# Group norm of a stem folded into per-image weights and biases, statistics taken in pairs of images, a chain's end moved into the next stage

## The chip, the core and the metric

One core of a Trainium2 chip. The metric is the device time of one execution in microseconds, the median of three runs. TensorE is written PE, VectorE DVE, ScalarE ACT, GpSimd POOL and the queue that issues transfers SP.

## What is computed

The input x is 8 images of 256 channels with 32x32 pixels. Only the first part of the reference matters here: a group norm without scale (32 groups of 8 channels), a 1x1 convolution to 128 channels with bias and SiLU, and, from the result, two chains of three 5x5 poolings.

```python
def _gn(v, G=32, eps=1e-05):
    ...
    return ((g - m) / jnp.sqrt(s + eps)).reshape(v.shape)
...
x_aux = _cbs(_gn(x), w_sta, b_sta)           # 1x1 convolution, bias, silu
for _ in range(3):
    y1.append(_tmaxavg(y1[-1]))              # 0.9 * max pool + 0.1 * mean pool
    y2.append(_rwpool(y2[-1]))               # sum(exp(x-c)*x) / (sum(exp(x-c)) + 1e-6)
```

The c of the second chain is the maximum over all eight images, so its first level can't start before all eight stem outputs are there. What follows (a 1x1 convolution of each chain, a gated stack of depthwise convolutions, a second group norm and attention per image) is the same in both kernels.

## The kernel before

The program is three blocks, one after the other, with a barrier of all engines between them. **The stem** (`phase_a`) makes the eight stem outputs, splits five weight matrices into a high and a low part (`k_w_hi`, `k_w_lo` and so on, for matrix multiplications in a reduced format), and already runs level 0 of the max-and-mean chain of image 0. **The level stage** (`phase_b`) runs the second chain for all images, 3 levels of 8 tiles, in 24 rounds s = 0 to 23, with two rounds of run-in (s = -2 and -1); beside it go levels 1 and 2 of image 0's max-and-mean chain. **The image stage** (`phase_c`) does the rest image by image; the change doesn't touch it.

Within a block every engine executes its own list in the order written; `wait_ge` on a semaphore is the only coupling. So the order in which a block's function writes an engine's steps decides what stands behind what.

In the stem, before: DVE takes `bn_stats` of four images (4 instructions of 128x512 each, `take_stats`), aggregates them (`bn_aggr`, `mv`), and in `deviations` exchanges with PE: PE averages the means over each group of 8 channels (`ps_mean`, a matmul with a block matrix), DVE forms the spread, PE averages that (`ps_var`), DVE adds epsilon, POOL raises to -1/2 (`rstd`), DVE forms the shift. Then `normalise(n)` writes xn = x * rstd + shift, two instructions of 128x1024, PE convolves xn (`convolve`, 4 fp32 matmuls of 128x512, seen in the trace as 8), ACT applies SiLU from PSUM into `x_all[:, n, 0]` (`silu`), DVE takes its maximum (`maximum`). The second four images follow in the same way. The weights to split are loaded into the half `x_all[:, :, 1]` of images that have been normalised, so SP waits for `xn_done` ahead of each. ACT makes the high parts (`split`), POOL the low ones (`low_parts`).

The chain of image 0 has for each level seven steps of `maxima` on DVE (steps 0 to 6; `pairs`, `work_a`, `tall`, `work_b`), six steps of `box_sum_step` on POOL (`zero`, `sum_a`, `sum_b`, `tall_sum`), a copy of the level into `zero` by ACT, and one `mixture` on DVE that writes the next level into `wide`. Before, DVE's step 0 and ACT's copy into `zero` of level 0 both read `wide[:, 0]`, which a transfer fills from `x_all[:, 0, 0]`.

In round s of the level stage DVE executes `product(s + 1)`, `residual(s)`, `improve(s)`, `divide(s)` and then one step of the chain; PE `sum_ey(s)`, `turn(s + 2)`, `sum_e(s + 1)`; ACT `estimate(s)` (a Ln and an Exp), possibly `product_hi(s + 1)`, and `exponent(s + 2)`; POOL `product_low(s + 1)` (writes `ey_lo`) and `e_low(s + 2)` (writes `e_lo`), then a box step. A tile m in `WHOLE` has its product summed by PE in full fp32, with no `product_hi` and `product_low`; `WHOLE` is set to the rounds in which POOL has box steps. At s = 8 and 16 a level starts: `reduce_tile`, `spread_max` on PE, `reduce_batch` and `set_eps` pass the maximum on.

## Time and profile before

| | us |
|---|---|
| median of 3 runs (lowest, highest) | 1432.04 (1429.85, 1433.74) |
| the profiled execution's own time | 1429.68 |
| its span in the trace | 1427.9 |
| stem, span start to the first instruction of the level stage | 0 to 87.4 |
| level stage, to the end of its last `divide` | 87.4 to 260.2 |
| image stage | 260.2 to 1427.9 |
| busy over the span | PE 1273.4, DVE 1148.8, ACT 704.6, POOL 159.5 |

A busy time is the sum of an engine's instructions. The duration of an instruction in the trace holds also the time in which it was issued but could not yet run, so the same form can show 1.2 us in one place and 4.4 us in another; the stages are therefore read from the timelines, not from the sums.

### The profile page before, as it was taken

What the parts mean: (1) busy time and instruction counts of PE and PEld (TensorE: products, weight loads), DVE (VectorE), ACT (ScalarE), POOL (GpSimd) and SP (SyncE); (2) the same over time, 40 slices, a digit from 0 to 9 for tenths busy, and PEclk for the clock granted to TensorE, in tenths of its full rate; (3) what the DMA queues carried; (4) which work ended last, traced back from release to release, by engine and by line L of the source; (5) the groups of instructions that cost most, each with busy time, mean ns of one, the idle gap of its engine ahead of it and who ended that gap; (6) DMA issues with size and microseconds to landing.
All of it is one profiled execution on the core that took longest, in us unless ns stands there. A gap on an engine that the chain in (4) does not pass through costs nothing.

```text
span 1427.9 us, 18374 instructions
## 1 busy us (share of the span) xinstructions
PE 1273.4 (89%) x7162; PEld 1063.4 (74%) x7162; DVE 1148.8 (80%) x1217; ACT 704.6 (49%) x762; POOL 159.5 (11%) x76
## 2 busy tenths in 40 slices
PE   3569899836999998999899989999999999999697
PEld 1249899524878877987798679868986898688597
DVE  7879888595899879877987799779987988786443
ACT  0256768550365347435653566346534653564243
POOL 1657677100000000000000000000000000000000
PEclk9879999867999999999999999999999999999899
DMA  7311212110000100020002000200020002000000
GB/s 291 147 45 75 89 75 106 42 59 0 30 15 1 75 29 15 0 73 29 15 0 103 0 15 15 88 15 0 15 88 15 0 15 88 0 1 36 25 1 30
DMA packets 19176, 62.84 MB, mean 44 GB/s; under 512 B 1601, under 2 KB 4289, under 8 KB 19137
## 3 DMA queue, kind: packets, MB, share of 16 engines
q1 hardware_dynamic: 18432, 62.00, 11.5%
q8 instruction: 27, 0.44, 0.1%
q10 hardware_dynamic: 704, 0.30, 0.1%
q14 instruction: 13, 0.10, 0.0%
HBM read 36.61 MB, written 25.17 MB: 43 GB/s over the span
## 4 chain that ended last, share of the span: by engine, by line
PE 59%; issue 14%; DVE 14%; ACT 6%; DMA 0%; DVEq 0%; ACTq 0%; POOLq 0%; POOL 0%
PE slot L1126 21%; PE slot L1164 12%; PE ps_o L1164 9%; DVE between L1439 5%; PE slot L549 3%; PE slot L1180 3%; DVE a L1439 2%; PE slot L1104 2%; PE ps_e L549 2%; PE ps_ey L565 2%; PE slot L1151 1%; PE ps_ey L549 1%; DVE ps_e L766 1%; DVE x_all L773 1%; PE ps_t L642 1%
## 5 line engine op out<-in xcount | busy, mean ns | idle before, releaser
L1164 PE MATMUL slot<-f_all,q_all 128*128 128x512 f32 x768 | 195.4, 406 | 13.4 <-ACT pooled L1305 13.4
L1164 PE MATMUL ps_o<-v_all,pt_all 128*128 128x256 f32 x1536 | 199.1, 286 | 5.4 <-ACT mixed L1324 5.2
L1164 PEld LDWEIGHTS ps_o<-v_all,pt_all 128*128 128x128 f32 x1536 | 188.7, 191 | 7.7 <-DVE pt_all L1443 6.2
L1164 PEld LDWEIGHTS slot<-f_all,q_all 128*128 128x128 f32 x768 | 144.1, 193 | 43.6 <-ACT pooled L1305 14.8
L1439 DVE SCALAR_TENSOR_TENSOR a<-between,k_columns,a 128x992 f32<-128x992 f32 (+1 forms) x128 | 157.4, 1231 | 4.9 <-ACT a L1296 2.6
L1056 POOL TENSOR_TENSOR c_rstd<-c_spread,k_minus_half 128x2 f32<-128x2 f32 x8 | 5.6, 697 | 1087.0 <-DVE gmean L1509 1087.0
L1319 ACT CAST v_all<-y 128x1024 fp32r<-128x1024 f32 x32 | 33.7, 1052 | 184.6 <-DVE y L1470 184.6
L1443 DVE TENSOR_TENSOR pt_all<-slot,pt_all 128x1024 fp32r<-128x1024 f32 x64 | 78.1, 1221 | 46.9 <-ACT pt_all L1310 46.9
L1104 PE MATMUL slot<-wide,k_cv 128*128 128x512 f32 x256 | 114.3, 597 | 0.0
L1324 ACT ACTIVATE mixed<-ps_o,row_inv 128x256 f32<-128x256 f32 x64 | 30.3, 473 | 150.1 <-PE ps_o L1164 150.1
L1296 ACT ACTIVATE a<-between,k_columns 128x1024 f32<-128x1024 f32 x64 | 79.4, 1241 | 48.6 <-DVE between L1439 47.7
L1448 DVE TENSOR_REDUCE c_minus_max<-slot 128x1 f32<-128x1024 f32 x64 | 78.1, 1220 | 10.3 <-PE slot L1164 10.3
L1104 PEld LDWEIGHTS slot<-wide,k_cv 128*128 128x128 f32 x256 | 47.5, 190 | 51.4 <-issue 50.7
L1439 DVE SCALAR_TENSOR_TENSOR between<-y,k_columns,between 128x992 f32<-128x992 f32 x64 | 79.4, 1250 | 7.6 <-ACT between L1296 6.5
L1310 ACT CAST pt_all<-slot 128x1024 fp32r<-128x1024 f32 x64 | 65.0, 1015 | 37.2 <-PE slot L1180 37.0
L1305 ACT ACTIVATE pooled<-slot,c_minus_max 128x1024 f32<-128x1024 f32 x64 | 71.6, 1119 | 21.5 <-DVE c_minus_max L1448 21.5
L1470 DVE SCALAR_TENSOR_TENSOR y<-slot,k_columns,y 128x1024 f32<-128x1024 f32 x32 | 41.0, 1281 | 50.0 <-PE slot L1126 35.1
L1439 DVE SCALAR_TENSOR_TENSOR between<-a,k_columns,between 128x960 f32<-128x960 f32 x64 | 77.2, 1215 | 1.1
L1289 ACT ACTIVATE y<-slot,k_columns 128x1024 f32<-128x1024 f32 x32 | 35.4, 1105 | 81.6 <-PE slot L1126 81.6
L1180 PE MATMUL slot<-k_ident,pooled 128*128 128x128 f32 x512 | 66.9, 273 | 4.0 <-ACT pooled L1305 4.0
L738 POOL TENSOR_TENSOR e_lo<-x_all,e_hi 128x1024 fp32r<-128x1024 f32 x24 | 61.5, 2563 | 47.6 <-ACT e_hi L693 47.6
L1126 PE MATMUL slot<-f_all,k_c_hi 128*128 128x512 f32 x232 | 64.0, 397 | 2.5 <-DVE y L1470 2.5
(166 smaller groups left out, 2725.0 us busy)
## 6 DMA issues: line engine op xcount, KB each, us to landing
levels<-x_all SPq DMA_DIRECT2D x32, 512.0 KB, 2.6
x_all<-in_x SPq DMA_DIRECT2D x8, 1024.0 KB, 13.3
q_all<-levels SPq DMA_DIRECT2D x8, 1024.0 KB, 4.9
x<-in_x SPq DMA_DIRECT2D x8, 1024.0 KB, 4.9
out<-x SPq DMA_DIRECT2D x8, 1024.0 KB, 3.9
pooled<-levels SPq DMA_DIRECT2D x8, 512.0 KB, 3.3
wide<-levels SPq DMA_DIRECT2D x7, 512.0 KB, 3.2
x_all<-in_w_c SPq DMA_DIRECT2D x2, 512.0 KB, 3.6
```

Source lines behind the costliest of these rows:

```text
L549: last = nc.tensor.matmul(out[:, r0 * W:r1 * W], part[:, k * P:(k + 1) * P], box[:, c0:c0 + (r1 - r0) * W], start=(b not in started), stop ...
L738: nc.gpsimd.tensor_tensor(e_lo[:, u], e[u], e_hi[:, u].bitcast(F32), ALU.subtract).then_inc(e_lo_done, 1)
L1104: last = nc.tensor.matmul(slot[:, h * HALF:(h + 1) * HALF], keep["cv1"][:, k, cols(m)], rows, start=(k == 0), stop=(k == KT - 1))
L1126: last = nc.tensor.matmul(slot[:, hs], weights[:, k], inputs(k)[:, hs], start=(at == 0), stop=(at == len(uses) - 1))
L1164: last = nc.tensor.matmul(out, lhs, rhs, start=(n == 0), stop=(n == len(parts) - 1))
L1180: last = nc.tensor.transpose(slot[:, cols(m)], prob[:, cols(m)], keep["ident"][:, :])
L1296: nc.scalar.activation(dst, src, ACT.Identity, scale=keep["taps"][:, s, c, 1:2], bias=keep["b_taps"][:, s, c:c + 1]).then_inc(taps_centre. ...
L1305: nc.scalar.activation(prob[:, :], slots_of["s", t][:, :], ACT.Exp, bias=minus_max[:, t:t + 1], accum_out=row_sum[:, t:t + 1]).then_inc(pr ...
L1310: nc.scalar.copy(pt_hi[:, t % 2], slots_of["t", t][:, :]).then_inc(pt_hi_done.sem, 1)
L1439: nc.vector.scalar_tensor_tensor(o, u, keep["taps"][:, s, c, tap:tap + 1], o, ALU.mult, ALU.add).then_inc(taps.sem, 1)
L1443: nc.vector.tensor_tensor(pt_lo[:, t % 2], slots_of["t", t][:, :], pt_hi[:, t % 2].bitcast(F32), ALU.subtract).then_inc(pt_lo_done.sem, 1)
L1448: nc.vector.tensor_reduce(minus_max[:, t:t + 1], slots_of["s", t][:, :], AX, ALU.max, negate=True).then_inc(maxed.sem, 1)
```

## The change

- `xn` and `normalise` are gone. For each image ACT multiplies the stem's weights by rstd (`weigh`: `w_image`, 128x128, two for an image), PE multiplies the stem's weights by the shifts (`biases`: `ps_bias`, 128x2 for a pair of images) and ACT adds `b_sta` (`b_image`). PE convolves `x_all` itself with `w_image`; `silu` uses `b_image`.
- Statistics, deviations, variances and powers go in four pairs of images instead of two fours (`PAIR = 2`). On PE the small matmuls of the next pair stand between the convolutions of this pair: means behind the first image, variances behind the first half of the second, biases behind its second half.
- The five weight matrices have buffers of their own (`raw_...`, loaded behind x with no wait), and ACT splits them late in its list.
- `zero` of level 0 is copied from `x_all` and not from the transferred `wide`; POOL's six box steps of level 0 stand between the powers, before the low parts.
- On DVE steps 0 to 3 of level 0's maxima stay in the stem; step 4 stands in round s = -1 and steps 5, 6 and the mixture in round s = 0 of the level stage. Levels 1 and 2 start one round later, and `WHOLE` moves by one.

```diff
-STAGED = {"w1": (0, 1, 0, 512), "w2": (0, 1, 512, 1024), "cvend": (1, 2, 0, 1024), "c1": (2, 4, 0, 1024), "cv2": (4, 5, 0, 1024)}
+PAIR = 2
...
+            for k in SPLIT:
+                sp.dma_start(raw[k][:, :, :], rows(k)).then_inc(weights_in[k], 16)
...
-            for k in SPLIT:
-                sp.wait_ge(xn_done, STAGED[k][1] * CT)
...
+            def weigh(g):
+                act.wait_ge(rstd_done, g + 2)
+                for n in images(g):
+                    for t in range(CT):
+                        at = n * CT + t
+                        nc.scalar.activation(w_image[:, n, t], w_sta[:, t], ACT.Copy, scale=rstd[:, at:at + 1]).then_inc(weighted_done, 1)
+                act.wait_ge(bias_sum_done, g + 1)
+                part = slice(g * PAIR, (g + 1) * PAIR)
+                nc.scalar.activation(b_image[:, part], ps_bias[:, part], ACT.Identity, bias=keep["b_sta"]).then_inc(bias_done, 1)
...
+            for g in range(groups):
+                first, second = images(g)
+                convolve(first, 0)
+                convolve(first, 1)
+                if g + 1 < groups:
+                    means(g + 1)
+                convolve(second, 0)
+                if g + 1 < groups:
+                    variances(g + 1)
+                convolve(second, 1)
+                if g + 1 < groups:
+                    biases(g + 1)
...
             inverse_deviations(0)
             inverse_deviations(1)
-            chain.box_sums(pool, 0, 0)
-            low_parts(("w1", "w2"))
-            low_parts(("cvend", "c1", "cv2"))
+            box_sum_steps(0, 1)
+            inverse_deviations(2)
+            box_sum_steps(2, 3)
+            inverse_deviations(3)
+            box_sum_steps(4, 5)
...
-WHOLE = frozenset([*range(1, 7), *range(11, 17)])
+WHOLE = frozenset([*range(2, 8), *range(12, 18)])
...
+                if s == -1:
+                    chain.maxima(dve, 0, 0, 4)
+                if s == 0:
+                    chain.maxima(dve, 0, 0, 5, 6)
+                    chain.mixture_of_sums(dve, 0)
...
-                if 0 <= s < 7:
-                    chain.maxima(dve, 0, 1, s)
-                if s == 8:
+                if 1 <= s < 8:
+                    chain.maxima(dve, 0, 1, s - 1)
+                if s == 9:
                     chain.mixture_of_sums(dve, 1)
-                if 9 <= s < 15:
-                    chain.maxima(dve, 0, 2, s - 9)
-                if s == 17:
+                if 10 <= s < 16:
+                    chain.maxima(dve, 0, 2, s - 10)
+                if s == 18:
                     chain.maxima(dve, 0, 2, 6)
                     chain.mixture_of_sums(dve, 2)
```

What stands in DVE's list from the statistics of the last images to the end of the stem, before (L471 is `take_stats`, L506 `maximum`, L501 `normalise`, L224, L203 and L230 the chain):

```order
L506 TENSOR_REDUCE rmc<-x_all 128x1
L493 SCALAR_TENSOR_TENSOR shift<-ps_mean,rstd 128x8
L501 TENSOR_SCALAR xn<-x_all,rstd,shift 128x1024 x2
L224 TENSOR_TENSOR pairs<-wide 128x32x31
L203 COPY pairs<-wide 128x32x2
L506 TENSOR_REDUCE rmc<-x_all 128x1
L501 TENSOR_SCALAR xn<-x_all,rstd,shift 128x1024 x2
L506 TENSOR_REDUCE rmc<-x_all 128x1
L224 TENSOR_TENSOR work_a<-pairs 128x1024
L224 TENSOR_TENSOR tall<-work_a,pairs 128x1024
L501 TENSOR_SCALAR xn<-x_all,rstd,shift 128x1024 x2
```

And now (L506 is `take_stats`, L512 the aggregation, L518 to L522 `deviations`, L527 epsilon, L532 the shift, L536 `maximum`, L223 and L202 the chain):

```order
L506 BN_STATS stats<-x_all 128x6 x4
L512 BN_AGGR mv<-stats 128x2 x4
L536 TENSOR_REDUCE rmc<-x_all 128x1
L518 TENSOR_TENSOR dev<-mv,ps_mean 128x4
L520 TENSOR_TENSOR dev<-dev 128x4
L522 TENSOR_TENSOR spread<-dev,mv 128x4
L527 TENSOR_SCALAR spread<-ps_var 128x4
L223 TENSOR_TENSOR pairs<-wide 128x32x31
L532 SCALAR_TENSOR_TENSOR shift<-ps_mean,rstd 128x4
L536 TENSOR_REDUCE rmc<-x_all 128x1
L202 COPY pairs<-wide 128x32x2
L223 TENSOR_TENSOR work_a<-pairs 128x1024
```

The exchange of the last images with PE and POOL now ends a few instructions ahead of the stem's end, and the passes that wrote xn are gone.

POOL's list from the powers on, before:

```order
L449 TENSOR_TENSOR rstd<-spread,k_minus_half 128x8 x2
L187 TENSOR_TENSOR sum_a<-zero 128x1088
L187 TENSOR_TENSOR sum_b<-sum_a 128x1024
L187 TENSOR_TENSOR tall_sum<-sum_b,zero 128x1024
L187 TENSOR_TENSOR sum_a<-tall_sum 128x1088
L187 TENSOR_TENSOR sum_b<-sum_a 128x1024
L187 TENSOR_TENSOR sum_b<-sum_b,tall_sum 128x1024
L456 TENSOR_TENSOR k_w_lo<-x_all,k_w_hi 128x512 x2
```

And now, from the third power on to the end of the stem:

```order
L480 TENSOR_TENSOR rstd<-spread,k_minus_half 128x4
L186 TENSOR_TENSOR tall_sum<-sum_b,zero 128x1024
L186 TENSOR_TENSOR sum_a<-tall_sum 128x1088
L480 TENSOR_TENSOR rstd<-spread,k_minus_half 128x4
L186 TENSOR_TENSOR sum_b<-sum_a 128x1024
L186 TENSOR_TENSOR sum_b<-sum_b,tall_sum 128x1024
L496 TENSOR_TENSOR k_w_lo<-raw_w,k_w_hi 128x512 x2
L496 TENSOR_TENSOR k_cvend_lo<-raw_cvend,k_cvend_hi 128x1024
L496 TENSOR_TENSOR k_c_lo<-raw_c,k_c_hi 128x2048
L496 TENSOR_TENSOR k_cv_lo<-raw_cv,k_cv_hi 128x1024
```

Two box steps and all low parts stand behind the last pair's power.

DVE's list at the start of the level stage, before (L761 is `product`, L766 `residual`, L773 `improve`, L782 `divide`):

```order
L761 TENSOR_TENSOR x_all<-ps_t,x_all 128x1024 x2
L766 SCALAR_TENSOR_TENSOR ps_e<-ps_e,eps,x_all 128x1024
L773 SCALAR_TENSOR_TENSOR x_all<-ps_e,x_all 128x1024
L782 ISA x_all,rmc<-x_all,ps_ey 128x1024
L782 ISA rmc 128x1
L224 TENSOR_TENSOR pairs<-wide 128x32x31
```

And now (L805, L810, L817 and L826 are the same four):

```order
L805 TENSOR_TENSOR x_all<-ps_t,x_all 128x1024
L223 TENSOR_TENSOR work_a<-tall 128x1088
L805 TENSOR_TENSOR x_all<-ps_t,x_all 128x1024
L223 TENSOR_TENSOR work_b<-work_a 128x1024
L223 TENSOR_TENSOR work_b<-work_b,tall 128x1024
L229 SCALAR_TENSOR_TENSOR wide<-sum_b,work_b 128x1024
L810 SCALAR_TENSOR_TENSOR ps_e<-ps_e,eps,x_all 128x1024
L817 SCALAR_TENSOR_TENSOR x_all<-ps_e,x_all 128x1024
```

Four chain instructions stand ahead of the first `residual`, and the one that stood behind the first `divide` has moved behind the second.

## Rows read from the trace of the kernel before

**Rows 1.** Windows of stem, level stage and image stage: window, length, busy by engine, clock, DMA

```profile
0.00:87.40 87.40, 37.16 (x72) 15.62 (x72) 71.33 (x92) 18.01 (x21) 36.66 (x20) 0.89 0.50 191
87.40:260.20 172.80, 157.13 (x1158) 151.81 (x1158) 141.51 (x136) 118.61 (x113) 117.25 (x48) 0.93 0.20 80
260.20:1427.90 1167.70, 1079.06 (x5932) 895.95 (x5932) 935.99 (x990) 567.96 (x629) 5.58 (x8) 0.97 0.08 28
```

**Rows 2.** Groups of the stem, one line of DVE: busy, mean ns, idle before

```profile
L501 DVE TENSOR_SCALAR xn<-x_all,rstd,shift 128x1024 f32<-128x1024 f32 x16 | 21.3, 1380 | 1.9 <-PE ps_a L426 1.8
```

**Rows 3.** Timeline of DVE in the stem: start, duration, idle before it

```profile
12.15 5.03 DVE L471 BATCH_NORM_STATS2 stats<-x_all 128x6 f32<-128x512 f32 x8 [0.33 <-DMA x_all<-in_x]
...
18.68 0.16 DVE L482 TENSOR_TENSOR dev<-mv,ps_mean 128x8 f32<-128x8 f32 x1 [0.75 <-PE ps_mean L415]
...
33.62 1.52 DVE L501 TENSOR_SCALAR xn<-x_all,rstd,shift 128x1024 f32<-128x1024 f32 x2
...
48.72 1.19 DVE L224 TENSOR_TENSOR pairs<-wide 128x992 f32<-128x992 f32 x1 [5.27 <-DMA wide<-x_all]
...
61.40 5.59 DVE L501 TENSOR_SCALAR xn<-x_all,rstd,shift 128x1024 f32<-128x1024 f32 x2
...
84.76 2.35 DVE L506 TENSOR_REDUCE rmc<-x_all 128x1 f32<-128x1024 f32 x2
```

**Rows 4.** Timeline of POOL in the stem

```profile
20.24 1.64 POOL L449 TENSOR_TENSOR rstd<-spread,k_minus_half 128x8 f32<-128x8 f32 x1 [17.40 <-DVE spread L488]
...
60.47 3.22 POOL L187 TENSOR_TENSOR sum_b<-sum_a 128x1024 f32<-128x1024 f32 x1
...
78.06 3.33 POOL L456 TENSOR_TENSOR k_cv_lo<-x_all,k_cv_hi 128x1024 fp32r<-128x1024 f32 x1
```

**Rows 5.** The page's groups, one line: a power of two columns in the image stage

```profile
L1056 POOL TENSOR_TENSOR c_rstd<-c_spread,k_minus_half 128x2 f32<-128x2 f32 x8 | 5.6, 697 | 1087.0 <-DVE gmean L1509 1087.0
```

**Rows 6.** Timeline of ACT: SiLU of image 0, three 256-column products, a one-column Exp

```profile
29.78 1.12 ACT L384 ACTIVATE x_all<-ps_a,k_columns 128x1024 f32<-128x1024 f32 x1 [25.59 <-PE ps_a L426]
...
50.75 1.01 ACT L397 ACTIVATE k_cv<-k_cv 128x256 f32<-128x256 f32 x3
...
96.78 0.29 ACT L713 ACTIVATE eps<-batch_max,eps_shift 128x1 f32<-128x1 f32 x1
```

**Rows 7.** Timeline of PE in the stem: three convolutions, one mean

```profile
24.16 12.45 PE L426 MATMUL ps_a<-xn,w_sta 128*128 128x512 f32 x24 [4.28 <-DVE xn L501]
38.32 0.39 PE L415 MATMUL ps_mean<-mv,k_group 128*128 128x8 f32 x2 [1.71 <-DVE mv L479]
```

**Rows 8.** Timeline of DVE in the level stage

```profile
95.83 1.23 DVE L761 TENSOR_TENSOR x_all<-ps_t,x_all 128x1024 f32<-128x1024 f32 x1 [3.21 <-ACT x_all L691]
100.05 1.29 DVE L766 SCALAR_TENSOR_TENSOR ps_e<-ps_e,eps,x_all 128x1024 f32<-128x1024 f32 x1 [3.00 <-ACT x_all L708]
...
103.79 2.81 DVE L224 TENSOR_TENSOR pairs<-wide 128x992 f32<-128x992 f32 x1
...
118.39 1.22 DVE L224 TENSOR_TENSOR work_a<-pairs 128x1024 f32<-128x1024 f32 x1
...
144.75 2.59 DVE L224 TENSOR_TENSOR work_b<-work_b,tall 128x1024 f32<-128x1024 f32 x1
```

**Rows 9.** Timeline of POOL in the level stage

```profile
92.52 2.36 POOL L738 TENSOR_TENSOR e_lo<-x_all,e_hi 128x1024 fp32r<-128x1024 f32 x1 [11.13 <-ACT e_hi L693]
...
97.16 2.41 POOL L738 TENSOR_TENSOR e_lo<-x_all,e_hi 128x1024 fp32r<-128x1024 f32 x1
...
118.50 3.34 POOL L738 TENSOR_TENSOR e_lo<-x_all,e_hi 128x1024 fp32r<-128x1024 f32 x1 [3.10 <-ACT e_hi L693]
```

**Rows 10.** Groups of the level stage, one line of POOL

```profile
L743 POOL TENSOR_TENSOR ey_lo<-x_all,ey_hi 128x1024 fp32r<-128x1024 f32 x12 | 28.7, 2388 | 8.6 <-ACT ey_hi L699 8.5
```

**Rows 11.** Timeline of PE: the same step of two successive rounds

```profile
125.31 3.65 PE L565 MATMUL ps_ey<-box,x_all 128*128 128x192 f32 x20
...
131.94 3.66 PE L565 MATMUL ps_ey<-box,x_all 128*128 128x192 f32 x20
```

More of the change, by code:

```diff
@@ L142, in set_max_borders, with zero_first @@
         self.nc.vector.memset(self.tall[:, :, :], LOWEST).then_inc(self.borders, 1)
-    def zero_first(self, act):
-        wait(act, self.loaded, 0, 16)
-        self.zero_level(0)
+    def zero_first(self, first):
+        self.nc.scalar.copy(self.zero[:, :, 2:2 + W], first).then_inc(self.zeroed.sem, 1)
     def zero_next(self, act, level):
@@ L344, in phase_a, with images @@
         x_v = x.rearrange("b (t p) h w -> b p t (h w)", p=P)
-        group = B // 2
+        groups = B // PAIR
         def of_group(g):
-            return slice(g * group * CT, (g + 1) * group * CT)
+            return slice(g * PAIR * CT, (g + 1) * PAIR * CT)
+        def images(g):
+            return range(g * PAIR, (g + 1) * PAIR)
         def rows(k):
@@ new lines, in convolve @@
+            def convolve(n, h):
+                if h == 0:
+                    pe.wait_ge(weighted_done, CT * n + CT)
+                    pe.wait_ge(stem_done, n + 1)
+                for k in range(CT):
+                    last = nc.tensor.matmul(ps[:, n % 2, h * HALF:(h + 1) * HALF], w_image[:, n, k],
+                                            x_all[:, n, k, h * HALF:(h + 1) * HALF], start=(k == 0), stop=(k == CT - 1))
+                if h:
+                    last.then_inc(sta_done, 1)
@@ L430, in _ @@
             pe.sem_inc(sta_done, 2)
             pe.wait_ge(stem_done, 2)
-            statistics(0)
-            for n in range(group - 1):
-                convolve(n, n % 2)
-            statistics(1)
-            convolve(group - 1, (group - 1) % 2)
-            with pe.Fori(group // 2, B // 2) as pair:
-                for u in range(2):
-                    convolve(pair * 2 + u, u)
+            means(0)
+            variances(0)
+            biases(0)
+            for g in range(groups):
[10 more added lines that the diff above has]
+                    biases(g + 1)
@@ L450, in inverse_deviations, with box_sum_steps @@
                                         ALU.pow).then_inc(rstd_done, 1)
-            def low_parts(names):
-                for k in names:
-                    pool.wait_ge(split_done, list(SPLIT).index(k) + 1)
-                    nc.gpsimd.tensor_tensor(flat(keep[k + "_lo"], k), raw[k], flat(keep[k + "_hi"], k).bitcast(F32),
-                                            ALU.subtract).then_inc(low_done, 1)
+            def box_sum_steps(*steps):
+                for step in steps:
+                    chain.box_sum_step(pool, 0, 0, step)
@@ L749, in _ @@
                     e_low(s + 2)
-                for level, begin in ((1, 0), (2, 10)):
+                for level, begin in ((1, 1), (2, 11)):
                     if begin <= s < begin + 6:
```

174 lines of the change are left out of this document (95 added, 79 removed).

## Prediction

> **What bounds the kernel now.** First the windows of the three stages: stem 87.4 us, level stage 172.8, image stage 1167.7 [rows 1]. The change leaves the image stage as it is, so its 1167.7 stand. In the stem DVE has 71.3 of 87.4 us on its books, PE 37.2, POOL 36.7 [rows 1], and DVE also ends the stem: two `maximum` instructions from 84.76, 2.35 us long, up to 87.11 [rows 3]; the level stage begins 0.3 later. So the question is what DVE's 71 us are made of. The groups show `normalise` with 16 instructions, 21.3 us, 1380 ns each [rows 2], while two of them in a quiet place take 1.52 and two in another 5.59 [rows 3]. What differs is POOL: in the second place it runs a box step from 60.47 to 63.69 [rows 4]. The same is seen on the chain's steps: 1.22 us in one round, 2.81 and 2.59 in others [rows 8], and on POOL, whose `e_lo` takes 2.36 alone and 3.34 from 118.50, where DVE's `work_a` had begun at 118.39 and kept it out until 119.61 [rows 8, 9]. So a DVE instruction that reads SBUF only and a POOL instruction exclude each other as a whole, and who begins first goes first. An instruction of DVE with an input in PSUM isn't held up: the `product` at 95.83 keeps 1.23 us while POOL works from 92.52 to 99.57, but for moments [rows 8, 9].
>
> The Trainium skill, "SBUF — State Buffer", section "SBUF: two separate sides", states it as a rule: the port pair that DVE and GpSimd share is an exclusive lock, held for the whole instruction. It speaks against the parts of this change that put chain steps beside a busy POOL; what that would make of the time is the rival "in step" below. The trace agrees with it, with 5.59 against 1.52 us.
>
> In the level stage PE repeats its work every 6.63 us where it is the bound (131.94 less 125.31) [rows 11]; DVE's four instructions and one chain step come to about 4.9 and 1.2, so there a step costs nothing until it is locked out.
>
> **The stem after, by its longest path.** That path is no longer DVE's passes, but statistics of the last pair, its power, and POOL's list behind it. I follow it in time.
>
> Statistics are 2.47 us an image (5.03 for two) and keep up with the loads [rows 3]. Pair 0 is aggregated at 12.2. One turn DVE, PE, DVE costs 0.75 of waiting [rows 3], and there are two of them, with four small instructions of about 0.2; the power of 4 columns isn't in the trace: 8 columns take 1.64 [rows 4], 2 take 0.70 [rows 5], both ends of my bound, in between on the line 1.0. Together 3.4: shifts of pair 0 at 15.6. ACT's 128x128 products aren't there either: 0.29 for one column and 1.01 for three of 256 columns that follow each other [rows 6] bound them at 0.29 and 0.34; two of them free PE for image 0, so it starts at 16.2. The skill has a price for such a small instruction ("VectorE: DVE Perf Modes", the errata section: a ScalarE copy of 128 elements measured at 350 cycles, 0.29 us as an estimate); the sum would be the same by it.
>
> Image 0's convolution ran 5.6 us before (24.16 to SiLU at 29.78), the next ones about 3.4 each (12.45 for three) [rows 6, 7]. So image 0 is through at 21.8, and only then can PE do the means of pair 1, for which DVE has been waiting since 19.1: deviations from 22.5, a new idle of 3.4 us. Now DVE's list up to the last power: deviations and `maximum(0)` 1.8, epsilon, power and shift 1.6, images 4 and 5 with `maximum(1)` and aggregation 2.4 + 1.1 + 2.4 + 0.4, to 32.3; means and deviations of pair 2 1.3, half of image 6 1.2, to 34.8. Its variances stand on PE behind half of image 3, which can't begin before the means: 1.7 us at the upper clock, 2.8 or more if PE has fallen to the lower level in its gap, then 0.4 for the small matmul [rows 7]; so epsilon between 34.8 and 36.8, I take 35.9. Then power and shift 1.5, the rest of image 6 0.6, two maxima 2.3, image 7 2.4, aggregation 0.4, the exchange 1.7 and a power 1.0: 45.8.
>
> Behind that power POOL has two box steps (2.4 each), and 5,120 columns of low parts; at 2388 ns for 1024 columns [rows 10] these are 11.9, together 16.7 and 62.5. DVE's steps 1, 2 and 3 of the maxima fall beside them, each ahead of one POOL instruction: 0.2 + 1.2 + 1.2 = 2.6, so 65.1, with the barrier's 0.3 **65.4 for the end of the stem, 22.0 earlier**. The high parts, seven ACT instructions between SiLUs, PE's last two images (until about 53) and DVE's last maxima (about 56) end before POOL: they cost nothing as long as POOL's tail is there. The transfers are hidden as well: the stem's 191 GB/s on average become 255, half to two thirds of the engines' time [rows 1], and the wait of 5.27 for `wide` [rows 3] is gone, since step 0 comes at 45. Bounds: every wait for the lock and for PE's clock absent gives 62, both worse than taken 69.
>
> **The start of the level stage, shown on the old clock.** Old: `product(0)` ends at 92.6, `product(1)` 95.83, `residual(0)` 100.05 [rows 8]. POOL is busy almost without a gap in that place: `e_lo` from 92.52, `ey_lo`, `e_lo` from 97.16 to 99.57 [rows 9], and now a second `ey_lo` behind it, since tile 1 has left `WHOLE`. Step 4 of the maxima waits for `e_lo` (94.9) and ends at 96.1; `ey_lo` then runs to 98.5, step 5 to 99.7, `e_lo` to 102.1, step 6 to 103.3, `ey_lo` to 105.7, and the mixture to 106.9. `residual(0)` stands behind it: **6.9 late**. Round 0 loses its own chain step of 2.81, but the next round is then led by PE, which waits for `divide(0)` before `sum_ey(1)`: I take 6.0 late from round 2 on. That this is made good later is not to be had, since PE's 6.63 a round are the bound from there.
>
> **The shift by a round.** Step 6 of level 1 now stands in round 7, between `divide(7)` and the start of level 1 at s = 8, which DVE leads; before it stood in round 6, where of its 2.59 [rows 8] PE's 6.63 left 0.9 to pay (4.9 + 2.6 - 6.6). It is 1.2 alone and 2.6 locked out, so 0.3 to 1.7 net; I take 1.3. Step 5 of level 2 in round 15 likewise: 1.2. The other steps meet POOL in new places. Of the three chain steps in rows 8 two were locked out, by 1.6 and 1.4, and one went free; after a start that is late by another amount the meetings fall otherwise. Between none more (0) and six of the 13 rounds with a step paying 1.3 more (8) I take three rounds, 3.9, nearer to none, since PE's bound still hides 0.5 of a round. Level stage: 6.0 + 1.3 + 1.2 + 3.9 = **12.4 longer**, bounds 6 and 18.
>
> **Sum.** -22.0 + 12.4 = -9.6. The profiled execution took 1429.68, 2.4 below the median; the difference is made against its span (1427.9 becomes 1418.3) and applied to the median: 1432.0 - 9.6 = 1422.4, **1422**.
>
> **The rivals.**
> - *A clean level stage* (chance 0.25): the new phase happens to avoid the lock, and the last term is 0 or the start costs less. For it: the step at 118.39, which went free by being 0.11 ahead of POOL [rows 8, 9]. It gives -22.0 + 8.5 = -13.5 and, with 0.5 less at the start, 1418.
> - *The gain is eaten* (0.16): the pairs make a chain of eight small exchanges across four engines, PE's clock falls in its gaps and every late power is followed by POOL's 19 us. Stem 69 and level stage 16 longer give -2.4, 1430, which can't be told from no change (a measurement of this kernel tells about 0.3%, 4.3 us).
> - *In step, slower* (0.08): one mechanism, the lock. If in each of the 13 rounds with a chain step POOL's `e_lo` begins before DVE's step, the step takes 3.6 in place of 1.2, a round lasts 4.9 + 3.6 = 8.5 in place of 6.63, and 13 rounds lose 24; with the 8.5 of the start and the level starts, 33 against 22: +11, 1443. It decides by 0.11 us, the lead that DVE had at 118.39 [rows 8, 9]. Against it: a late DVE also delays ACT and POOL, so the phase should slip out again after a few rounds.
> - *The change doesn't remove DVE's work from the path* is excluded for the stem: the passes are gone from DVE's list and their place is with ACT, which has 18 of 87.4 us busy [rows 1].
>
> **How the numbers follow.** The forecast, 1419 to 1428, has 0.51. Faster by over 0.3%: forecast, clean stage and a little of the third, 0.77; within 0.3%: 0.15; slower: 0.08. The range leaves out the slower rival, the worst of the eaten gain and what lies near the two lower bounds together (stem 62, level stage 6 longer: -19.4, 1413), 0.2 in all: 1411 to 1431.
>
> **What would show it.** In the profile after: no `xn`; POOL's `k_cv_lo` as the last work of the stem, at 65; DVE idle from 19 to 22.5 before its second `dev`; the last power at 45 to 46; `residual(0)` 19.5 us behind the stage's start where it was 12.6; the level stage at 185, with a chain step before each level start. Wrong would be: a stem that DVE or ACT ends, a `residual(0)` that isn't late (the mixture not locked out), or an image stage that differs from 1167.7 by over 1.

## The result, and the profile after

The changed kernel takes 1425.69 us (median of 6 runs, 1421.97 to 1427.69) where the kernel before takes 1431.55 (6 runs, 1429.85 to 1433.74): 5.9 us less, ratio 0.9946 with a 95% interval of 0.9929 to 0.9963. That is faster, by a little more than the 0.3% that a measurement can tell from no change. Its profiled execution took 1425.96, span 1424.2, 3.7 below the span before. First the windows of the three stages of the changed kernel, cut where those of [rows 1] are (window, length, busy time and number of PE, PEld, DVE, ACT and POOL, granted clock, DMA share, GB/s):

```profile
0.00:64.22 64.22, 35.86 (x96) 17.22 (x96) 41.80 (x83) 22.69 (x40) 34.17 (x22) 0.95 0.68 260
64.22:254.82 190.60, 169.43 (x1158) 164.10 (x1158) 156.03 (x140) 119.77 (x114) 119.33 (x48) 0.87 0.18 72
254.82:1424.20 1169.38, 1080.10 (x5932) 896.75 (x5932) 936.05 (x989) 568.03 (x629) 5.59 (x8) 0.97 0.08 28
```

The stem lost 23.2 us, the level stage gained 17.8, the image stage 1.7: -3.7. In the level stage PE executes the same 1158 instructions, but they are 12.3 us longer and the clock is 0.87 where it was 0.93. That is the first hint of what the forecast had not priced.

**The stem.** On DVE the passes over xn are gone, and with them the 71.33 us of [rows 1]: 41.80 now. Its timeline, answering to [rows 3] (start, duration, idle before it):

```profile
22.54 0.16 DVE L518 TENSOR_TENSOR dev<-mv,ps_mean 128x4 f32<-128x4 f32 x1 [3.47 <-PE ps_mean L427]
...
43.50 1.18 DVE L223 TENSOR_TENSOR pairs<-wide 128x992 f32<-128x992 f32 x1
45.60 0.16 DVE L532 SCALAR_TENSOR_TENSOR shift<-ps_mean,rstd 128x4 f32<-128x4 f32 x1 [0.91 <-POOL rstd L480]
...
53.60 2.33 DVE L536 TENSOR_REDUCE rmc<-x_all 128x1 f32<-128x1024 f32 x2
64.22 0.16 DVE L832 TENSOR_REDUCE tile_max<-rmc 128x1 f32<-128x8 f32 x1 [8.29 <-PEq L295]
```

DVE is idle for 3.5 us before its second `dev`, because the means of pair 1 stand on PE behind all of image 0; and it has nothing to do for the last 8.3 us of the stem. POOL has, in its timeline:

```profile
14.44 1.01 POOL L480 TENSOR_TENSOR rstd<-spread,k_minus_half 128x4 f32<-128x4 f32 x1 [11.60 <-DVE spread L527]
...
43.66 1.90 POOL L480 TENSOR_TENSOR rstd<-spread,k_minus_half 128x4 f32<-128x4 f32 x1 [2.52 <-DVE spread L527]
45.54 2.36 POOL L186 TENSOR_TENSOR sum_b<-sum_a 128x1024 f32<-128x1024 f32 x1
47.98 2.35 POOL L186 TENSOR_TENSOR sum_b<-sum_b,tall_sum 128x1024 f32<-128x1024 f32 x1
50.29 4.52 POOL L496 TENSOR_TENSOR k_w_lo<-raw_w,k_w_hi 128x512 fp32r<-128x512 f32 x2
54.76 2.36 POOL L496 TENSOR_TENSOR k_cvend_lo<-raw_cvend,k_cvend_hi 128x1024 fp32r<-128x1024 f32 x1
57.07 4.51 POOL L496 TENSOR_TENSOR k_c_lo<-raw_c,k_c_hi 128x2048 fp32r<-128x2048 f32 x1
61.52 2.35 POOL L496 TENSOR_TENSOR k_cv_lo<-raw_cv,k_cv_hi 128x1024 fp32r<-128x1024 f32 x1
```

The last power ends at 45.6, and behind it POOL works without a gap to 63.87. The power of 4 columns costs 1.01, and 1.90 where DVE's `pairs` had begun 0.16 earlier.

**The level stage.** DVE at its start:

```profile
69.32 3.50 DVE L223 TENSOR_TENSOR work_a<-tall 128x1088 f32<-128x1088 f32 x1
72.75 1.21 DVE L805 TENSOR_TENSOR x_all<-ps_t,x_all 128x1024 f32<-128x1024 f32 x1
73.88 2.28 DVE L223 TENSOR_TENSOR work_b<-work_a 128x1024 f32<-128x1024 f32 x1
76.19 3.28 DVE L223 TENSOR_TENSOR work_b<-work_b,tall 128x1024 f32<-128x1024 f32 x1
79.58 3.19 DVE L229 SCALAR_TENSOR_TENSOR wide<-sum_b,work_b 128x1024 f32<-128x1024 f32 x1
82.81 1.29 DVE L810 SCALAR_TENSOR_TENSOR ps_e<-ps_e,eps,x_all 128x1024 f32<-128x1024 f32 x1
```

All four chain steps, worth 1.2 each when undisturbed, are locked out by POOL (they can't begin while an instruction of POOL runs) and show 12.3 together; `residual(0)` comes 18.59 after the start of the stage where it came at 12.62. To see where the rest goes, take the end of each `divide` (L826, L829) from the stage's start, in both kernels:

| round | before | after | later by | after, second profile (e10) | later by |
|---|---|---|---|---|---|
| 0 | 16.4 | 22.4 | 6.0 | 22.4 | 6.0 |
| 7 | 64.8 | 70.2 | 5.4 | 71.1 | 6.3 |
| 8 (level 1 starts) | 73.5 | 81.2 | 7.7 | 82.1 | 8.6 |
| 15 | 122.0 | 130.9 | 8.9 | 129.2 | 7.2 |
| 16 (level 2 starts) | 130.7 | 139.8 | 9.1 | 138.1 | 7.4 |
| 18 | 144.1 | 152.9 | 8.8 | 151.2 | 7.1 |
| 19 | 149.5 | 162.2 | 12.7 | 160.6 | 11.1 |
| 21 | 161.4 | 179.6 | 18.2 | 173.2 | 11.8 |
| 23 | 172.8 | 190.6 | 17.8 | 185.2 | 12.4 |

Over half of what the stage lost in the first profile is lost in rounds 18 to 21. Here are DVE and POOL of the changed kernel at round 18, where step 6 of level 2 and its mixture stand now:

```profile
217.05 3.06 DVE L223 TENSOR_TENSOR work_b<-work_b,tall 128x1024 f32<-128x1024 f32 x1
220.22 1.23 DVE L229 SCALAR_TENSOR_TENSOR wide<-sum_b,work_b 128x1024 f32<-128x1024 f32 x1
```

```profile
216.66 2.37 POOL L782 TENSOR_TENSOR e_lo<-x_all,e_hi 128x1024 fp32r<-128x1024 f32 x1
```

The same step met nobody in the profile of the kernel before:

```profile
223.22 1.22 DVE L224 TENSOR_TENSOR work_b<-work_b,tall 128x1024 f32<-128x1024 f32 x1
224.55 1.22 DVE L230 SCALAR_TENSOR_TENSOR wide<-sum_b,work_b 128x1024 f32<-128x1024 f32 x1
```

POOL had begun 0.39 before DVE, so DVE's step waited it out, the mixture and `product(19)` came behind, and PE, which waits for the product, stood idle. PE of the changed kernel there, with `turn` (L686) and the sums (L593):

```profile
222.85 1.94 PE L686 MATMUL ps_t<-k_ident,x_all 128*128 128x128 f32 x8 [3.08 <-DVE x_all L805]
224.44 2.43 PE L593 MATMUL ps_e<-box,e_hi 128*128 128x192 f32 x10
226.67 2.33 PE L593 MATMUL ps_e<-box,e_lo 128*128 128x192 f32 x10
...
233.07 1.91 PE L686 MATMUL ps_t<-k_ident,x_all 128*128 128x128 f32 x8
...
236.43 1.30 PE L593 MATMUL ps_e<-box,e_lo 128*128 128x192 f32 x10
```

After the idle 3.08 us the same ten matmuls take 2.33 instead of 1.30, until 236. The windows of this stretch say why; the granted clock, the last but two of a row, is 0.50, the lower level (1.2 GHz), for ten microseconds:

```profile
215.00:220.00 5.00, 3.97 (x33) 3.65 (x32) 4.96 (x3) 3.60 (x4) 4.03 (x2) 1.00 0.26 105
220.00:225.00 5.00, 2.15 (x10) 2.18 (x11) 4.83 (x5) 1.22 (x2) 1.14 (x1) 0.73 0.01 3
225.00:230.00 5.00, 5.00 (x26) 5.00 (x25) 2.52 (x3) 2.95 (x3) 3.60 (x2) 0.50 0.25 105
230.00:235.00 5.00, 5.00 (x25) 5.00 (x26) 3.65 (x3) 2.15 (x3) 2.37 (x1) 0.50 0.00 0
```

### The profile page after: what moved, and what is told of

Same layout as the page of the kernel before. It is cut to its first block, busy times and chain, and to the rows that moved or that the text cites. A ratio compares the mean times of both kernels' runs of the same rounds, so it can differ in the third digit from the quotient of the medians.

```text
span 1424.2 us, 18431 instructions
## 1 busy us (share of the span) xinstructions
PE 1285.4 (90%) x7186; PEld 1078.1 (76%) x7186; DVE 1133.9 (80%) x1211; ACT 710.5 (50%) x782; POOL 159.1 (11%) x78
## 4 chain that ended last, share of the span: by engine, by line
PE 60%; DVE 15%; issue 14%; ACT 5%; DMA 0%; DVEq 0%; ACTq 0%; POOLq 0%; POOL 0%
PE slot L1175 21%; PE slot L1213 13%; PE ps_o L1213 9%; DVE between L1488 5%; PE slot L593 3%; PE slot L1229 3%; DVE a L1488 2%; PE ps_e L593 2%; PE ps_ey L609 2%; PE slot L1153 2%; PE slot L1200 1%; PE ps_t L686 1%; PE ps_ey L593 1%; DVE ps_e L810 1%; DVE x_all L817 1%
## 5 line engine op out<-in xcount | busy, mean ns | idle before, releaser
L1213 PEld LDWEIGHTS slot<-f_all,q_all 128*128 128x128 f32 x768 | 145.1, 195 | 43.9 <-ACT pooled L1354 14.8
L1368 ACT CAST v_all<-y 128x1024 fp32r<-128x1024 f32 x32 | 33.7, 1053 | 185.6 <-DVE y L1519 185.6
L1497 DVE TENSOR_REDUCE c_minus_max<-slot 128x1 f32<-128x1024 f32 x64 | 78.1, 1220 | 11.1 <-PE slot L1213 11.1
L1488 DVE SCALAR_TENSOR_TENSOR between<-y,k_columns,between 128x992 f32<-128x992 f32 x64 | 79.4, 1250 | 6.9 <-ACT between L1345 5.8
L782 POOL TENSOR_TENSOR e_lo<-x_all,e_hi 128x1024 fp32r<-128x1024 f32 x24 | 62.5, 2605 | 50.7 <-ACT e_hi L737 50.6
## 6 DMA issues: line engine op xcount, KB each, us to landing
raw_c<-in_w_c SPq DMA_DIRECT2D x1, 1024.0 KB, 13.8
```

Source lines behind the costliest of these rows:

```text
L782: nc.gpsimd.tensor_tensor(e_lo[:, u], e[u], e_hi[:, u].bitcast(F32), ALU.subtract).then_inc(e_lo_done, 1)
L1213: last = nc.tensor.matmul(out, lhs, rhs, start=(n == 0), stop=(n == len(parts) - 1))
L1488: nc.vector.scalar_tensor_tensor(o, u, keep["taps"][:, s, c, tap:tap + 1], o, ALU.mult, ALU.add).then_inc(taps.sem, 1)
L1497: nc.vector.tensor_reduce(minus_max[:, t:t + 1], slots_of["s", t][:, :], AX, ALU.max, negate=True).then_inc(maxed.sem, 1)
```

## The experiments

The theory: the new stem is worth its 23 us whatever stands in the level stage; the part of the change that moves the chain's end into the stream costs more than it frees; and its late part is one lock wait in round 18, made dearer by the lower clock. The rivals: the two parts depend on each other (the stem is only short because the steps left it), or the level stage is longer because it begins at a lower clock, whatever its order. Eleven kernels were run, in three lots on three chips, each lot with its own runs of the kernel before (medians 1434.17, 1435.14 and 1435.80; one of the eleven runs behind the last took 4489.95 and is left out of the ratios). Totals are therefore compared within a lot (e1 to e4, e5 to e8, e9 to e11) or by their ratios. The diffs are against the changed kernel where nothing else is said.

**e1, the new stem with the old level stage.** Level 0 of the chain stays in the stem as a whole, ACT's copy of level 1 with it, and the rounds of levels 1 and 2 are those of the kernel before:

```diff
             maximum(6)
             maximum(7)
+            chain.maxima(dve, 0, 0, 4, 5, 6)
+            chain.mixture_of_sums(dve, 0)
...
-WHOLE = frozenset([*range(2, 8), *range(12, 18)])
+WHOLE = frozenset([*range(1, 7), *range(11, 17)])
```

> The changed stem, but level 0's steps 4 to 6 and its mixture back at the end of the stem's DVE list, and the level stage as it was before the change. Theory (the chain instructions ahead of the first residual, the locks behind them and the shift by a round cost the level stage 17.8 us): level stage back at 172.8 within 1.5; the four chain instructions fill DVE's idle time from 56 to 64 and each holds up one of POOL's low parts, so the stem ends at 68 to 70 instead of 64.2; span about 1410, median about 1412, 13 to 14 below the changed kernel. Rival (the level stage is slow because PE enters it after a longer idle stretch at the lower clock): level stage stays at 185 or more, median 1424 or above.

Measured: 1416.82, ratio 0.9872 (0.9849 to 0.9895), stem 71.1, `residual(0)` at 12.97, level stage 175.8: stem and level stage each over 1 us longer than expected. Without the stream part the change is worth more than with it. The stem's timeline on DVE shows what the four steps cost there:

```profile
56.72 2.45 DVE L223 TENSOR_TENSOR work_a<-tall 128x1088 f32<-128x1088 f32 x1
59.20 7.86 DVE L223 TENSOR_TENSOR work_b<-work_a 128x1024 f32<-128x1024 f32 x1
...
71.12 0.16 DVE L835 TENSOR_REDUCE tile_max<-rmc 128x1 f32<-128x8 f32 x1 [1.47 <-PEq L295]
```

Step 5 waits 6.6 us for POOL's last two low parts, so the stem is 6.9 longer than the changed kernel's, and the level stage 14.8 shorter (9.4 against the second profile). PE was idle for 17.0 us ahead of the level stage (11.0 in the changed kernel), so a longer idle time ahead of it doesn't by itself make the stage long.

This run also says what the wait of round 18 is not. Its level stage is 3.0 longer than before, in the same order. At the end of round 17 it is still 0.4 ahead (135.5 against 135.9), and then the mixture, in round 17 as before, is locked out:

```profile
207.87 3.23 DVE L229 SCALAR_TENSOR_TENSOR wide<-sum_b,work_b 128x1024 f32<-128x1024 f32 x1
```

```profile
212.50 1.06 PE L689 MATMUL ps_t<-k_ident,x_all 128*128 128x128 f32 x8 [2.65 <-DVE x_all L808]
```

From the end of `divide(17)` to the end of `divide(19)` it takes 16.9 us, and so it does in e5, e6 and e8, which have this order too (16.9 to 17.0), and in both profiles of the changed kernel (16.9). The 13.7 of the kernel before stand alone, in its one profile. So this wait is not the price of standing a round later: the two steps meet POOL in either place, and in the profile before they happened to pass. Of the 9.4 us by which the changed kernel's second profile is longer than e1's level stage, 8.1 are there at the end of round 17.

**e2, the old stem with the new level stage** (against the kernel before: only `WHOLE`, the steps in the rounds, and the steps 4 to 6 and the mixture out of the stem).

```diff
-            between = ((2, 3), (4,), (5, 6))
+            between = ((2,), (3,), ())
...
-            chain.mixture_of_sums(dve, 0)
...
+                if s == -1:
+                    chain.maxima(dve, 0, 0, 4)
```

> The stem of before without steps 4 to 6 and the mixture of level 0, and the changed level stage. Theory (the two halves of the change are independent): stem some 5 to 9 us shorter than 87.4, since DVE ends it and loses 4.41, 3.24 and 1.2 us plus step 4's 1.3; level stage 185 to 191; median 1436 to 1442, slower than before. Rival (the slow level stage comes from the new stem): level stage 173 to 178, median about 1427.

Measured: 1440.41, ratio 1.0057 (1.0034 to 1.0080), stem 79.4, level stage 188.0. By itself the stream part makes the kernel slower: 8.0 us off the stem, 15.2 onto the level stage. `residual(0)` comes at 18.60, as in the changed kernel, so the late start belongs to the order and not to the stem. Nor does it belong to the clock: e2 has the lower clock for the first 9 us of the stage and the changed kernel for the first 18, and the first two `divide` end at 22.4 and 28.5 in both. Together e1 and e2 say that the parts hardly depend on each other: their profiled spans are 12.1 less and 9.3 more than before, -2.8 together where the changed kernel has -3.7. The medians add up less sharply, 17.4 less and 6.2 more, -11.1, against the changed kernel's -5.9 on one chip and -14.3 on another (e10).

**e3, tile 1 kept in `WHOLE`**, so that POOL has one `ey_lo` less at the start.

```diff
-WHOLE = frozenset([*range(2, 8), *range(12, 18)])
+WHOLE = frozenset([*range(1, 8), *range(12, 18)])
```

> The changed kernel with tile 1 back among the tiles whose product PE sums in full fp32, so that POOL has no ey_lo for tile 1 at the start. Theory (the mixture of level 0 waits for that ey_lo, 79.58 to 81.7): the mixture takes 1.2 instead of 3.19 and residual(0) comes 2 us earlier, but the fp32 sum of tile 1 costs PE 3.5 instead of 2.3, so the second divide gains 0 to 1 us: median 1424 to 1427, hardly to be told from the changed kernel. Rival (the lock at this place costs nothing, PE at the lower clock is what is late): residual(0) unchanged.

Measured: 1421.44, ratio 0.9908 (0.9890 to 0.9926); `residual(0)` at 16.61, 2.0 earlier, since the mixture takes 1.23 where it took 3.19. Of the 6.0 us at the start, 2.0 are the `ey_lo` that tile 1 brought. How much of them lasts is open: the end of round 7 comes at 68.1 where the changed kernel has 70.2 and 71.1, that of round 18 at 151.4 where it has 152.9 and 151.2, and the stage takes 185.9, between 190.6 and 185.2. Its total can't be told from that of e10 below, since the two were run on different chips.

**e4, step 6 of level 2 in round 17**, the mixture alone in round 18.

```diff
-                if s == 18:
-                    chain.maxima(dve, 0, 2, 6)
+                if s == 17:
+                    chain.maxima(dve, 0, 2, 6)
+                if s == 18:
                     chain.mixture_of_sums(dve, 2)
```

> The changed kernel with step 6 of level 2's maxima in round 17 instead of 18; the mixture stays in 18. Theory (the step waited 1.8 us for POOL in round 18 with the mixture behind it, PE stood idle 3.08 us and then ran the next rounds at the lower clock, which cost 9 us between divides 18 and 21): level stage about 182, median 1417 to 1420. Rival (the late rounds are slow for another reason): level stage within 2 of 190.6.

Measured: 1421.03, ratio 0.9899 (0.9879 to 0.9920), level stage 184.8, between the theory's 182 and the rival's 188 or more, 5.8 less than in the changed kernel's first profile, all of it behind round 18. PE:

```profile
221.46 1.20 PE L686 MATMUL ps_t<-k_ident,x_all 128*128 128x128 f32 x8 [1.75 <-DVE x_all L805]
222.32 2.43 PE L593 MATMUL ps_e<-box,e_hi 128*128 128x192 f32 x10
224.54 1.84 PE L593 MATMUL ps_e<-box,e_lo 128*128 128x192 f32 x10
226.22 1.31 PE L593 MATMUL ps_ey<-box,ey_hi 128*128 128x192 f32 x10
```

The mixture is now the one locked out (3.08), PE is idle 1.75 instead of 3.08, and it is back at the upper clock after some 3 us. I read this as the edit's gain, until e10.

**e10, the changed kernel once more**, in another lot, since e4 stood against one profile of it.

> The changed kernel itself once more, beside the others on the same chip, to read their ratios against: 0.993 to 0.996 of before, level stage 186 to 192.

Measured: 1421.53, ratio 0.9908 (0.9888 to 0.9928), level stage 185.2, not 190.6; both lie outside what was expected. The lock wait is there again (3.11), and PE's idle time (3.10), but:

```profile
221.83 1.94 PE L686 MATMUL ps_t<-k_ident,x_all 128*128 128x128 f32 x8 [3.10 <-DVE x_all L805]
223.43 2.01 PE L593 MATMUL ps_e<-box,e_hi 128*128 128x192 f32 x10
225.27 1.31 PE L593 MATMUL ps_e<-box,e_lo 128*128 128x192 f32 x10
```

The upper clock is back at 225, after 3 us and not after 13. So round 18's wait costs 3.8 and 3.9 in the two profiles, against the one profile of before (round 19 lasts 9.3 where it lasted 5.4), and what follows costs 5.5 in the one and 0.8 in the other (up to round 21). e2, e3, e7 and e11 have the same two steps in round 18, so six traces can be set side by side (end of one `divide` to the end of another):

| | round 19 | 20 and 21 | 19 to 23 | lower clock |
|---|---|---|---|---|
| changed, first profile | 9.3 | 17.4 | 37.7 | 13 us |
| e3 | 9.3 | 14.3 | 34.6 | 6 us |
| changed again (e10), e2, e7, e11 | 9.3 | 12.7 to 12.9 | 33.7 to 34.0 | 3 to 4 us |
| e4 | 8.0 | 12.9 | 31.9 | 3 us |
| before | 5.4 | 11.9 | 28.7 | none |

The 13 us at the lower clock are the exception, one in six. e4's edit itself is worth 1.3 in round 19 and about 2 up to the end of the stage; the rest of its 5.8 is the exception that it was compared with. The same program has 1425.69 and ratio 0.9946 on one chip, 1421.53 and 0.9908 on another.

**e11, the first steps behind `divide`.** Steps 5, 6 and the mixture stand behind the first `divide` instead of ahead of `residual(0)`, and ACT's copy of level 1 a round later.

```diff
-                if s == 0:
-                    chain.maxima(dve, 0, 0, 5, 6)
-                    chain.mixture_of_sums(dve, 0)
...
+                if s == 0:
+                    chain.maxima(dve, 0, 0, 5, 6)
+                    chain.mixture_of_sums(dve, 0)
                 if 1 <= s < 8:
```

> The changed kernel with steps 5, 6 and the mixture of level 0 behind the first divide instead of ahead of the first residual (ACT's copy of level 1 a round later). Theory (the gap ahead of residual(0) isn't idle, because POOL holds the lock in it; what the chain instructions cost is their own time plus the locks, wherever they stand): residual(0) at 13 to 14.5 behind the stage's start instead of 18.6, first divide 5 earlier, but the divides from the third on at most 2 us earlier; level stage 187 to 191. Rival (the place ahead of residual(0) is what costs, since ACT, PE and the clock all wait for the first divide): level stage 182 to 185, the whole 5 to 6 us kept.

Measured: 1423.46, ratio 0.9916 (0.9895 to 0.9937), `residual(0)` at 13.28 and the first `divide` at 17.1, 5.3 earlier; the second at 26.5, only 2.0 earlier, and the fifth at 50.0, 1.2 earlier than in e10 beside it; the stage 187.1 against 185.2. The steps cost about the same behind `divide` as ahead of it: rounds 1 and 2 last 9.4 and 9.0 where e10 has 6.1 and 9.4, and round 3 7.9 where it has 6.6.

**e5 and e6, towards a better version.** e5 is e1 with `split` of w1, w2, cvend and c1 early in ACT's list and their low parts between POOL's powers. e6 is e5 with the low part of c1 on DVE, behind the mixture.

```diff
-            for n, k in enumerate(("w1", "w2", "cvend", "c1", "cv2")):
...
             box_sum_steps(0, 1)
+            low("w1", "w2")
             inverse_deviations(2)
             box_sum_steps(2, 3)
+            low("cvend")
             inverse_deviations(3)
             box_sum_steps(4, 5)
+            low("c1", "cv2")
```

```diff
             chain.mixture_of_sums(dve, 0)
+            dve.wait_ge(split_done, list(SPLIT).index("c1") + 1)
+            nc.vector.tensor_tensor(keep["c1_lo"][:, :, :], raw["c1"][:, :, :], keep["c1_hi"][:, :, :].bitcast(F32),
+                                    ALU.subtract).then_inc(low_done, 1)
```

> As e1 (changed stem with all of level 0 in it, level stage of before), but ACT splits w1, w2 and cvend behind the third SiLU and c1 behind the fifth, and POOL makes the low parts of w1 and w2 ahead of the third power and of cvend ahead of the fourth. Theory (POOL's tail behind the last power, shared under the lock with DVE's chain steps, ends the stem): 4.9 us of POOL's work move into gaps in which it waited, and the stem ends at 66 to 67 instead of 71.1, the level stage stays at 173 to 176; median 4 to 5 us below e1's ratio, about 0.984 of before. Rival (DVE's own list ends that stem): stem at 70 or more, no gain.

> As e5, with the low part of c1 (2048 columns) on DVE at the end of its list instead of on POOL. Theory (a lock, so what counts is the sum of both engines' exclusive times): POOL's 4.5 us become about 2.3 on DVE, the stem ends at 64 to 66, 1 to 2.5 below e5. Rival (two engines that only wait for their own work): DVE's list gets longer by 2.3 and ends the stem 2 us later than in e5.

Measured: e5 1414.35, ratio 0.9849 (0.9833 to 0.9866), stem 67.5 (3.6 below e1's), level stage 175.1; e6 1412.59, ratio 0.9839 (0.9823 to 0.9856), stem 67.0, level stage 177.5. e6 is 22.6 us below the kernel before and the fastest of all, though not told apart from e5 beside it. Its profiled execution is its slowest (1419.04), so the 177.5 may be above what it has in most. Its timeline on DVE and POOL:

```profile
64.33 2.29 DVE L588 TENSOR_TENSOR k_c_lo<-raw_c,k_c_hi 128x2048 fp32r<-128x2048 f32 x1
66.95 0.16 DVE L843 TENSOR_REDUCE tile_max<-rmc 128x1 f32<-128x8 f32 x1 [0.32 <-PEq L295]
```

```profile
56.93 2.37 POOL L491 TENSOR_TENSOR k_cv_lo<-raw_cv,k_cv_hi 128x1024 fp32r<-128x1024 f32 x1 [5.33 <-ACT k_cv_hi L395]
```

DVE makes in 2.29 what took POOL 4.51, but then DVE's list ends the stem and POOL waits for ACT's last high part: the stem gained 0.6 where some 4 were taken off POOL, less than the theory's 1 to 2.5 and not the 2 more of the rival.

**e7, fours instead of pairs**, the fold kept; the lists of the stem are put in the order that this needs.

```diff
-PAIR = 2
+PAIR = 4
```

> The changed kernel with statistics and powers in two fours of images instead of four pairs (PAIR = 4; the group norm still folded into weights and biases). It tells what the pairs give by themselves. Theory: the first convolution starts at 22 instead of 16, but the exchanges in the middle fall away and the last power comes at about the same time, 44 to 48; stem 66 to 70 instead of 64.2, level stage 186 to 191, median 2 to 5 us above the changed kernel. Rival (the pairs are what shortens the stem): stem at 76 or more.

Measured: 1425.80, ratio 0.9938 (0.9921 to 0.9955), stem 67.4, level stage 184.7. So the pairs as written here, with the lists that go with them, are worth 2.5 to 3.2 us of stem (against 64.85 and 64.22). The other 20 come from what the two have in common: the fold, the buffers of the weights and the steps that left.

**e8, eight matmuls of 512 columns behind PE's last convolution**, on e6, to hold the clock over the barrier. They write a buffer that nobody reads.

```diff
+            for n in range(8):
+                nc.tensor.matmul(ps_warm[:, :], w_sta[:, 0, :], x_all[:, 0, 1, 0:HALF], start=True, stop=True)
```

> As e6, and PE does eight fp32 matmuls of 128x512 behind the last convolution, whose result nobody reads (some 7 us), so that it enters the level stage without its long idle stretch. Theory: the first rounds of the level stage run at the upper clock, its turns take 1.04 instead of 1.9 and its sums 1.3 instead of 2.3; the first divide comes 1 to 3 us earlier, and the level stage ends at most 3 us earlier. Rival (the start of the level stage is bound by ACT and DVE alone): the first divide unchanged at 16.4 to 16.8 us behind the stage's start.

Measured: 1434.77, ratio 0.9998 (0.9984 to 1.0012). Stem 67.4 and level stage 175.1 (e6: 67.0 and 177.5). The filler ends at 62, PE is idle for another 5.5 us, and its first step is as slow as without it, 1.91 in both; the upper clock is back earlier, the first sum of `e_lo` taking 1.30 at 76 where e6 has 2.34, and `residual(0)` comes at 12.3 instead of 13.8. The 2.4 us of level stage can't be put down to that, since e5 has the same 175.1 without a filler. Yet the kernel is 22 us slower than e6, and that in the image stage, which nobody touched; it is told at the end.

**e9, the mixture of level 2 in round 18**, on e6.

```diff
                 if s == 17:
                     chain.maxima(dve, 0, 2, 6)
+                if s == 18:
                     chain.mixture_of_sums(dve, 2)
```

> As e6, with the last mixture of the chain in round 18 instead of 17 (the step ahead of it stays in 17). Theory (two chain instructions in one round hold the next product and with it PE's turn back by about 2.7 us, and PE then runs at the lower clock): the 7.5 us between divides 18 and 19 become 5.5 to 6.5, the level stage ends at 172 to 175 instead of 177.5, median 2 to 4 us below e6's ratio: about 0.982 of before. Rival (those rounds are slow without it): level stage within 1.5 of 177.5.

Measured: 1414.93, ratio 0.9865 (0.9843 to 0.9887), level stage 175.0 where e6's is 177.5. Up to round 17 the two level stages are the same within 0.1; round 18 ends 2.4 earlier, round 19 2.1 and the stage 2.5. Round 19 itself, expected at 5.5 to 6.5, lasts 8.0 (7.6 in e6). The ratio doesn't show the gain, and the two profiles are the slowest execution of the one and the fastest of the other: inconclusive for the total. PE is idle for 1.74 us there and keeps the upper clock, where it lost it behind 1.75 in e4.

## Why the prediction was right, and where it was not

The forecast was 1422, 9.6 us less; it came out at 1425.69, 5.9 less, inside the range and on the side that had 0.77. By its steps:

- *The stem by its longest path:* right, in mechanism and size. Forecast 65.4, 22.0 earlier; measured 64.2, 23.2 earlier. The first idle of DVE ends at 22.5 as forecast, the last power at 45.6 (forecast 45.8), POOL's tail follows to 63.9. The three DVE steps beside the tail were priced at 2.6, one for each to get between POOL's instructions; POOL's rows show 18.3 from the last power to the end of its list where 16.7 is the undisturbed sum, so 1.6. The power of 4 columns was taken at 1.0 between two bounds and is 1.01.
- *The products on ACT:* 0.29 and 0.34 were the bounds for a 128x128 product. Four of them show 1.28, 0.32 each. Image 0's convolution began at 16.6 (forecast 16.2) and ended at 22.4 (21.8).
- *The start of the level stage:* right. `residual(0)` forecast at 19.5 and 6.9 late, measured at 18.6 and 6.0 late; from round 2 on 6.0 as forecast (5.4 to 6.3 in round 7), and not made good. e11 shows one other order that doesn't get it back, and e3 that 2.0 of it are the tile that left `WHOLE`.
- *The shift by a round:* 1.3 and 1.2 forecast; measured 2.3 at s = 8 and 0.2 at s = 16, in both profiles. 2.5 in both, the sum right, the parts not.
- *"The other steps meet POOL in new places", 3.9:* **this is the term that was mis-sized.** It was built as three of 13 rounds that pay 1.3 more. Its model can be set against DVE's timeline of the whole stage: of the 16 chain instructions behind the first four, 5 are held up in the kernel before, by 6.9 us together, and 5 in the changed one, by 9.3 (against 1.22 undisturbed, and 0.22 for the copy of 64 columns). So the locks themselves grew by 2.4, less than the 3.9; in the second profile only 3 are held up, by 5.1, less than before. The length of the locks is therefore not what the stage lost. In rounds 9 to 15 the loss came out at 1.2 (and at -1.4 in the second profile), and then 3.8 in round 19 alone, behind round 18, where step 6 and the mixture stand behind each other and the first is held up by 1.8. That loss is measured against a profile of the kernel before in which the two steps passed; e1, e5, e6 and e8 lose as much over rounds 18 and 19 with them in the old place. What had no term is what followed: PE idle for 3.1 us, and its clock at the lower level for up to 13 us, which cost 5.5 us in the first profile and 0.8 in the second. The level stage was forecast 12.4 longer; it is 17.8 longer in the one and 12.4 in the other. That the second meets the forecast is partly luck: 3.9 in one round where 3.9 stood for three. The clock was in the stem's steps (as 1.7 or 2.8 for half an image) and in no step of the level stage.
- *The image stage:* "wrong if it differs by over 1" was too narrow a test. It differs by 1.7. None of the kernels touches it, and over their profiles (e8 aside) it goes from 1167.7 (before, e9) to 1172.8 (e6). Nothing in these runs ties such a difference to an edit.
- *The rivals:* "clean level stage" didn't come, and "in step, slower" didn't either: 11 of those 16 instructions are undisturbed, so the phase slips out again, as was argued. "The gain is eaten" had the right place, but the wrong cause: not the exchange of the pairs (the stem is early), but the lock waits at the start and in round 18, and the clock. The rule of the Trainium skill that spoke against the change ("SBUF — State Buffer", "SBUF: two separate sides") is borne out by the four steps at the start, 12.3 us instead of 4.9. The whole of the move was measured by e2: 15.2 us on the level stage for 8.0 off the stem. The forecast had these inside its 12.4 and 22.0 and did not ask what each half was worth alone, and so did not see that half of the change is a loss.

How well the total fits is less sure than the terms. The same program stood 5.9 below the kernel before on one chip and 14.3 (ratio 0.9908) on another; 9.6 lies between. The 5.4 us between its two profiles in the level stage explain some of that. The rest is open, for the kernel before was traced on the first chip alone.

## What to carry to other kernels

When a step moves from a place where it ends a stage into a stream that is bound by another engine, price the whole of its lock-outs there and run each half of the change alone: here the new stem was worth 17 us by itself (e1; 12 in the profiled spans), and the move gave back 4 to 8 of them (profiled spans of 1419.8 and 1424.2 against 1415.8). A wait of DVE for POOL can cost more than its length, as here, where 1.8 us of it stopped PE for 3.1 and its clock then stood at the lower level; so look for places where two such steps stand in a row ahead of the product that PE waits for. Before an edit's gain is believed, profile the same program twice, the kernel before too.
